# A depthwise 3x3 convolution in fp32: four taps on TensorE and five on VectorE, against nine taps on TensorE in 64x64 quarters of its array

## The reference

```
h   = relu(bn1(depthwise_conv3x3(layernorm_over_channels(x)) + dw_b))   # 9 taps, one weight per channel and tap
h   = where(max|h| over an image's channel < 4.0, 0, h)
h   = relu(bn2(conv1x1(h) + pw_b));  h = where(max|h| < 0.001, 0, h)
x   = x + h
t   = tokens(x)                                  # 16*784 = 12544 rows of 128
t   = t + moe(layernorm(t))                      # 8 experts, each takes its 1024 best tokens
                                                 # (softmax over the tokens), 128 -> 512 -> gelu -> 128
out = from_tokens(t)
```

## Time and profile before

| | |
|---|---|
| median of 3 runs | 505.8 us (504.53 to 506.65) |
| span of the profiled execution | 502.9 us |
| TensorE busy (matmuls) | 361.9 us, 72% |
| VectorE busy | 327.1 us, 65% |
| ScalarE busy | 274.3 us, 55% |

### The profile page before, as it was taken

One profiled execution on the slowest core, in us unless ns is written; L12 is line 12 of the kernel. 1 busy time (PEld: TensorE's weight loads), 2 busy tenths in 40 slices (PEclk: granted clock), 3 DMA queues, 4 the chain that ended last, 5 costly groups with the idle time before them and its releaser, 6 DMA issues. The chain is left out here.

```text
span 502.9 us, 6936 instructions
## 1 busy us (share of the span) xinstructions
PE 361.9 (72%) x1947; PEld 255.7 (51%) x1947; DVE 327.1 (65%) x1004; ACT 274.3 (55%) x587; POOL 159.3 (32%) x151
## 2 busy tenths in 40 slices
PE   4989888888889985631021798999990498876575
PEld 3656555566666553520011374677560467464453
DVE  5699988888889898578879548556620025235444
ACT  3577888888888876677640528556551240510000
POOL 4000000000000000000005777787888788876000
PEclk9999999999999997655555799999997598997755
DMA  4604555555554342479101223344443267847998
GB/s 103 188 38 141 185 168 185 167 185 168 185 182 150 130 131 96 137 238 392 71 1 33 55 56 94 95 65 64 83 85 34 55 189 134 194 61 169 285 390 344
DMA packets 36396, 72.01 MB, mean 143 GB/s; under 512 B 6385, under 2 KB 16785, under 8 KB 36369
## 3 DMA queue, kind: packets, MB, share of 16 engines
q1 hardware_dynamic: 24256, 56.52, 35.0%
q0 software_dynamic: 9472, 8.66, 11.2%
q10 hardware_dynamic: 2640, 6.51, 3.3%
HBM read 34.96 MB, written 30.29 MB: 130 GB/s over the span
## 5 line engine op out<-in xcount | busy, mean ns | idle before, releaser
L403 POOL DMA_INDIRECT picked<-token_rows,slot_idx x32 | 31.5, 986 | 270.7 <-issue 270.4
L691 PE MATMUL psC<-x_pad,tap_diag 128*128 128x392 f32 x256 | 90.8, 498 | 6.7 <-ACT x_pad L570 5.6
L1009 DVE SCALAR_TENSOR_TENSOR conv<-x_pad,taps_w,conv 128x784 f32<-128x784 f32 x64 | 65.9, 1030 | 0.8
L691 PEld LDWEIGHTS psC<-x_pad,tap_diag 128*128 128x128 f32 x256 | 46.1, 189 | 37.0 <-DVE conv L1009 5.1
L1302 DVE TENSOR_TENSOR y_sum<-psC,b_rows 128x512 f32<-128x512 f32 x15 | 10.4, 692 | 75.2 <-PE psC L869 75.2
L869 PE MATMUL psC<-w,hid 128*128 128x128 f32 x480 | 56.6, 280 | 2.2 <-ACT hid L633 2.1
L869 PEld LDWEIGHTS psC<-w,hid 128*128 128x128 f32 x480 | 55.8, 197 | 4.6 <-issue 3.0
L613 ACT ACTIVATE picked_T<-psA 128x512 f32<-128x512 f32 x16 | 9.0, 594 | 59.9 <-PE psA L836 59.9
L426 POOL DMA_INDIRECT moe_sum_late<-y_rows,slot_idx x24 | 37.9, 1581 | 9.5 <-issue 7.0
L483 ACT ACTIVATE rows<-psD,sm 112x128 f32<-112x128 f32 x98 | 35.7, 464 | 9.3 <-DVE sm L1001 9.3
L729 PE MATMUL psB<-act,pw_masked 128*128 128x392 f32 x64 | 27.9, 563 | 17.0 <-DVE pw_masked L1085 17.0
(11 more groups left out here) (211 smaller groups left out, 728.8 us busy)
## 6 DMA issues: line engine op xcount, KB each, us to landing
token_rows<-rows SPq DMA_DIRECT2D x16, 416.5 KB, 3.6
x_in<-in_x_dram SPq DMA_DIRECT2D x16, 392.0 KB, 3.5
x_res<-in_x_dram SPq DMA_DIRECT2D x16, 392.0 KB, 4.3
moe_sum<-zero_rows SPq DMA_DIRECT2D x16, 392.0 KB, 4.9
x_all<-x SPq DMA_DIRECT2D x16, 392.0 KB, 2.9
moe_sum_late<-zero_rows SPq DMA_DIRECT2D x16, 392.0 KB, 7.7
out_dram<-act ACTq DMA_DIRECT2D x16, 392.0 KB, 6.2
w<-in_L_ffn_W_dram SPq DMA_DIRECT2D x16, 256.0 KB, 3.3
```

Of the source, the lines that this page charges most:

```text
L403: nc.gpsimd.indirect_dma_start(out=picked_in[k][:, b, :], out_offset=None, in_=rows_dram, in_offset=bass.IndirectOffsetOnAxis(ap=slot_idx[ ...
L691: ins = nc.tensor.matmul(psC[:, h, 0:HALF].rearrange("c (h w) -> c h w", w=W), tap_diag[:, n, :], x_pad_v[:, q, y0:y0 + LINES, dx:dx + W], ...
L1009: return nc.vector.scalar_tensor_tensor(o, x_pad_v[:, q, y0 + dy:y0 + dy + lines, dx:dx + W], taps_w[:, PE_TAPS + n:PE_TAPS + n + 1], acc, ...
```

## The change

All nine taps are matmuls on TensorE. The array is used in four quarters of 64 x 64. `x_pad` holds each image twice: lines 0 to 15 with channels in their places, and the lines from 12 on with the two halves of the channels exchanged. The upper half image goes from partitions 0-63 to 0-63 and 64-127 to 64-127; the lower one, stored exchanged, goes from 0-63 to 64-127 and from 64-127 to 0-63, which brings its channels back. So a tap is four matmuls of 64 rows, 64 columns and 392 moving columns, one in each quarter. Two matmuls write the two partition halves of bank 0 of `psC`, and two those of bank 1. ScalarE reads both banks of `psC` at once for bn1. VectorE no longer adds taps; it makes the exchanged copy (two instructions of 64 partitions and 448 elements out of `psB`) and takes the norm of the rows (7 instructions of 112 x 128 out of `psD`), which was ScalarE's. The set-up builds 18 weights of 128x64 where it built 4 of 128x128, after two more small loads. Each image's stage 1 now has x turned in step k, its norm in step k+1, the taps in step k+2; the stages behind are as far on as before. The buffer of zeros lies in `hid`, so ScalarE waits for the last store of zeros before the experts. The exchange of `psD`, `psA` and `psC` at both ends is gone: stage 1 has `psA`, stage 6 has `psD`, always.

```diff
-PE_TAPS = 4
+HC = C // 2
+KEPT = 16
+PART = (KEPT + 1) * PW
-        tap_diag = sb("tap_diag", [128, PE_TAPS, 128])
+        tap_diag = sb("tap_diag", [128, 9, HC])
+        tap_turned = sb("tap_turned", [128, 9, HC])
-        x_pad = sb("x_pad", [128, 2, (H + 2) * PW])
+        x_pad = sb("x_pad", [128, 2, 2 * PART])
...
+            sp.dma_start(taps_turned[0:HC, :], taps_d[HC:C, :]).then_inc(s_prm, 16)
+            sp.dma_start(taps_turned[HC:C, :], taps_d[0:HC, :]).then_inc(s_prm, 16)
...
-            def conv_half(img, q, h):
-                if since(img, 1):
-                    pe.wait_ge(s_taken, img * 2 + h - 1)
-                for n in range(PE_TAPS):
+            def conv_taps(img, q):
+                pe.wait_ge(s_pad, img + 1)
+                pe.wait_ge(s_turn, img + 1)
...
+                if since(img, 1):
+                    pe.wait_ge(s_h1, img)
+                for n in range(9):
                     dy, dx = TAPS[n]
-                    y0 = h * LINES + dy
-                    ins = nc.tensor.matmul(psC[:, h, 0:HALF].rearrange("c (h w) -> c h w", w=W), tap_diag[:, n, :],
-                                           x_pad_v[:, q, y0:y0 + LINES, dx:dx + W],
-                                           start=(n == 0), stop=(n == PE_TAPS - 1))
+                    for half, weights, lines in ((0, tap_diag, x_pad_v), (1, tap_turned, x_turned_v)):
+                        for row in range(2):
+                            of = slice(row * HC, row * HC + HC)
+                            col = row if half == 0 else 1 - row
+                            y0 = dy + half
+                            ins = nc.tensor.matmul(psC[col * HC:col * HC + HC, half, 0:HALF].rearrange("c (h w) -> c h w", w=W),
+                                                   weights[of, n, :], lines[of, q, y0:y0 + LINES, dx:dx + W],
+                                                   start=(n == 0), stop=(n == 8))
                 ins.then_inc(s_conv, 1)
...
+                    for a, tiles in enumerate((range(4), range(3, TPI))):
+                        pe.wait_ge(s_n1, img * 2 + a + 1)
...
+                    for t in range(TPI):
+                        ins = nc.vector.tensor_scalar(rows[:, q5, t * ROW:t * ROW + C], row_tiles[:, t, :],
+                                                      row_sm[:, 5, t:t + 1], row_sm[:, 6, t:t + 1], ALU.mult, ALU.add)
...
+                    dve.wait_ge(s_t2, img1 * 2 + 2)
+                    for to, of in ((0, HC), (HC, 0)):
+                        ins = nc.vector.tensor_copy(x_turned_v[to:to + HC, q1, 0:KEPT, 1:1 + W],
+                                                    psB[of:of + HC, 1, 0:KEPT * W].rearrange("c (h w) -> c h w", w=W))
+                    ins.then_inc(s_turn, 1)
```

More of the change, by code:

```diff
@@ L460, in _ @@
             nc.scalar.activation(warm[:, :], eps_c[:, :], ACT.Sqrt)
[L462 to L469, removed]
             def step(pair, u):
-                onN, imgN, _, _ = image(pair, u, -1)
+                k = pair * 2 + u
+                on1, img1, q1, _ = image(pair, u, 1)
                 on2, img2, q2, _ = image(pair, u, 2)
                 on3, img3, q3, _ = image(pair, u, 3)
[L475 to L487, removed]
+                on5, img5, _, _ = image(pair, u, 5)
+                if on3:
                     if since(img3, 2):
@@ L572, in step @@
-                if on:
-                    roots()
-                if on2 and not ending:
-                    first_signs()
+                if on1:
+                    if isinstance(img1, int) and img1 == 0:
+                        act.wait_ge(s_const, 1)
+                    if since(img1, 2):
+                        act.wait_ge(s_conv, img1 - 1)
+                    act.wait_ge(s_t2, img1 * 2 + 1)
+                    nc.scalar.activation(x_pad_v[:, q1, 1:1 + KEPT, 1:1 + W],
+                                         psB[:, 0, 0:KEPT * W].rearrange("c (h w) -> c h w", w=W), ACT.Copy).then_inc(s_pad, 1)
@@ new lines, in step @@
+                on, img, q, use = image(pair, u, 0)
+                if on:
+                    pe.wait_ge(s_xin[q], use * 16 + 16)
+                    for a, tiles in enumerate(BANK_TILES):
+                        if since(img, 1):
+                            pe.wait_ge(s_n1, img * 2 + a - 1)
+                        for t in tiles:
+                            ins = nc.tensor.transpose(ln_tiles[:, t, :], x_in[:, q, t * P:(t + 1) * P], ident[:, :])
+                        ins.then_inc(s_t1, 1)
@@ L1087, in step @@
-                onN, imgN, _, _ = image(pair, u, -1)
-                now = columns(on0, on5)
-                now_ln, now_row = img0 if on0 else None, img5 if on5 else None
-                new = columns(onN, on4)
-                new_ln, new_row = imgN if onN else None, img4 if on4 else None
-                def keep_second():
+                if on1 or on5:
+                    now = columns(on1, on5)
+                    inverse(img1 if on1 else None, img5 if on5 else None, now)
+                    shift(k - 1, now)
@@ L1171, in _ @@
+                if on4:
+                    stats(row_tiles, TPI, s_m3, img4, s_t3)
+                if on0 or on4:
+                    new = columns(on0, on4)
+                    moments_a(img0 if on0 else None, img4 if on4 else None, new)
+                    moments_b(k, new)
+                    moments_c(k, new)
+                if isinstance(img0, int) and img0 == 0:
+                    setup_first()
             steps(dve, step)
```

396 lines of the change are left out of this document (140 added, 256 removed).

## The result

The changed kernel takes **521.1 us** (median of 4 runs, 520.4 to 522.4); the kernel before took 506.2 beside it (4 runs, 504.5 to 507.4). The ratio is **1.031, interval 1.027 to 1.035**: slower, by 15 us, where 4 were forecast. The profiled span grew by 17.7 us, from 502.9 to 520.6.

A forecast was written before the change was run, and what follows sets the result against it. The prediction saw two close bounds: TensorE's own work and VectorE's in-order work gating `pw_masked`. It added 8.5 us until the last tap, took off 4.9 behind it: 505.8 + 3.6 = 509.4, with store contention 510, range 497 to 614.

The forecast's parts named there:

- the rival at 605: Taps on TensorE: records start only in program order, 36 slots, 11.9 us an image, +95, 605 us; chance 0.27.
- quarters side by side: Taps on TensorE: the four quarters run at once, 5.94 us an image; kernel at 497 to 520 us; chance 0.56.
- The taps: TensorE, each image: 72 records in four parallel quarters take 18 slots of 0.330, 5.94 us, plus 0.2 for drains.
- one bank at a time: Taps: two row halves of the array can't write one bank together, 17.8 us an image, +190, 700 us; chance 0.05.
- no overlap: Taps: no quarter runs beside another, 23.8 us an image, +286, 796 us; chance 0.05.
- partly hidden: Taps: weight loads or drains between quarters only partly hidden, 7 to 10 us an image, 525 to 575 us; chance 0.07.
- The gate: VectorE's path from the end of the taps to the next step's 1x1 convolution: 4.2 us, setting a step of 11.75.
- The clock at the start: Image 0's taps: begin at 16.3 us for 14.54 and run at 0.33 a slot; step 3 begins at 26.7.
- Up to image 15's convolution: Start and steps: last taps end at 197.7, 8.5 us later than before; relu, count and mask then need 3.1.
- The end: From image 15's 1x1 convolution to the turn of the logits: 16.4 us where it was 12.8, rows in series through `psD`.
- The rest: From the turn of the logits on, both kernels do the same; the 3.6 us lost by then is carried over.
- The rival that ended faster: Step: a gate of 3.9 downward lets TensorE's own work set 11.2 us, with an end of 15; 500 us; chance 0.14.

The follow-up runs named there:

- experiment 2: Changed kernel with the same 36 tap matmuls per image reordered: quarter by quarter, 768.1 us; two quarters in turn, then the other two, 598.0 us.
- norm_one: Changed kernel with the norm of an image's rows as one instruction instead of seven, first tile's scale for all: 518.2 us, ratio 1.027 to the kernel before.
- Experiment 3: Changed kernel with `keep` and `pw_masked` moved ahead of the stats of x on VectorE: 507.9 us, ratio 1.006 to the kernel before.
- experiments 4 and 6: Changed kernel, two separate edits: image 14's rows turned into `psA`, 517.2 us; set-up split with tap weights built first, 520.9 us.
- experiment 7: Changed kernel with mask moved ahead, image 14's rows in `psA` and set-up split: 499.2 us; with ten idle TensorE matmuls at the start too: 498.7 us.
- setup_split: Second of experiments 4 and 6: changed kernel with tap weights built first, other set-up after the first image's stats: 520.9 us, ratio 1.031.

## Why the prediction was right, and where it was not

- **The number: in the range, but with luck.** 521.1 lies within 497 to 614 only because the range reached up to the rival at 605. For quarters side by side, which is what came, the prediction gave 497 to 520, and that is just missed: slower was right, but by 15 us and not by 4. The mechanism of the step was right; the start and the end were sized too small.
- **The taps: right.** 18 slots of 0.330 and 0.2 for the drain were 6.14; 6.09 was measured. This was called the weakest step, with 0.44 on other outcomes. All four of those rivals (in program order, one bank at a time, no overlap, partly hidden) fall with the 6.1 us. The Trainium skill, in TensorE: Matmul & The Clock Gate, Part 3, The mechanism, has matmuls start strictly in program order; experiment 2 shows records of another quarter ahead of waiting ones, so here the measurement decides against it. The rule on banks in the Trainium skill, in TensorEngine Tiling, Gotcha 1: PSUM Pressure, that different row tiles can't use one PSUM bank at the same time, does not hold here for two row halves that write different partitions of one bank: their records start 7 ns apart.
- **The gate: right, each part a little too small.** The copies took 1.26 to 1.29 (1.2), the mask and what follows 0.69 (0.62), the turn 1.02 (0.95), the convolution ahead of the taps 1.51 (1.42), the stats 1.40 as forecast. The step is 12.1 where 11.75 stood. From the first 1x1 convolution to that of step 16 (29.0 to 186.7) it is 157.7 us where 152.8 stood: 3.5 of the 4.9 are the steps.
- **The clock at the start: not in the sum.** The prediction took the taps of image 0 at 0.33 a slot, because the kernel before ran them so the earlier trace rows. They ran at 0.65 until 21 us, which makes 2.2 of the 2.3 us by which the first convolution is late; the stretch from 41.5 to 44.9 makes step 4 13.5 us long, 1.4 more.
- **Up to image 15's convolution** the forecast came to 197.7 + 3.1 = 200.8, no change to before. Measured 207.6: 2.3 from the start, 1.4 from the second stretch, 3.5 from the steps, and -0.4 in the last two.
- **The end: mis-sized, and one wait was not seen.** 16.4 us from that convolution to the turn of the logits was forecast, 21.3 measured. That image 15's rows wait in `psD` for the norm of image 14's was foreseen. That image 14's rows wait in the same way for the norm of image 13's was not: TensorE stands 3.87 us ahead of 213.05, and from the convolution to that turn it is 5.46 us, where it was 2.77. `norm_one` shows this wait to be real, since the stretch shrinks by just what the norm there is shorter. From image 14's turn to image 15's it is 9.0 us for 3.5, and from there to the logits 6.8 for 6.6. The norm, in both links, was taken as 1.4 and is 2.32. At the lower clock each image's row turns and logits take 1.74 and 2.65 us instead of 0.98 and 1.45 at the full clock, some 2.0 for each image; but the kernel before had part of this end at the lower clock too (its 1x1 convolution took 2.98 us, not 1.58), so how much of the missing 4.9 is the clock's is not shown. In `norm_one`, where image 14's rows were turned at the full clock (0.98 us, logits 1.81), the 9.0 are 6.3: 1.1 less by the norm and 1.6 by the clock.
- **The rest.** Of the 17.7 us of span 15.3 are there at the turn of the logits, against 3.6 forecast; the 11.7 between are 6.8 up to image 15's convolution and 4.9 behind it. The last 2.4 arise in the second part, where both kernels do the same work. The granted clock is at the lower level at other times there in the two traces. That this makes the 2.4 is likely, but no run was made for it.
- **The rival that ended faster** was ruled out by its own condition: the gate is 4.4, not under 3.9, since the copies are no cheaper than 0.62 each. Experiment 3 meets the condition in another way, by taking the stats out of the gate; it gets the step of 11.2 that this rival had, and with experiments 4 and 6 the kernel is 1.3% faster than before. So the idea of the change was sound; what kept it from paying was the place of one small instruction in VectorE's program, an end that was put in series, and a start in which TensorE stood still.

## What to carry to other kernels

When work is moved off an engine whose program runs in order, look first at where the instruction that the next engine waits for stands in what is left: here two instructions of 0.13 and 0.29 us stood behind 1.4 us of stats in every step, and moving them gave 12.7 us in a kernel that had lost 15. Compare the steady step, the start and the end with the kernel before one by one: the step was hardly longer, and what could be gained in it hid that the loss lay at the ends. Matmuls in quarters of the array paid off fully here when neighbours in the program named different quarters. Waits of TensorE in the fill can be paid twice, as the wait and as matmuls at the lower clock behind it (experiment 7); at the end of the chain the two stand together as well, and 1.6 us of it show in `norm_one`.

## What the hardware showed that was not expected

- TensorE does not start records strictly in program order when they are in different quarters: the first of a waiting quarter passed three records of each quarter ahead of it at a seam, and no more, with one quarter at a time and with two in turn (20.1 and 10.7 us for 72 records that take 6.1 with all four in turn).
- On VectorE, scaling 112x128 out of `psD` with two values per partition takes 0.32 us from one to the next ((2.32 - 0.40)/6), 401 ns each, where the stats of the same shape take 0.20; as one instruction of 896 columns it is 1.20 instead of 2.32.
- A start with more waiting kept TensorE at half speed until 21.0 us, where it had been fast by 14.4; ten useless matmuls ahead made it fast by 12.0, when seven x turns took 0.93 us for the 1.70 of the kernel after. Later a wait of 2.48 us was followed by matmuls at the lower level from 41.5 to 44.9 us, an equal one 12 us earlier was not, and in `setup_split`, with two waits of 2.47, both were.
